# A two-layer block of linear attention and an fp8 product on one core: the last full unit's bias and final sums on DVE instead of POOL, and new orders of work at both ends

## The reference

```python
x = x + attn(layernorm(x))
x = x + ffn(layernorm(x))

def attn(h):                       # 8 heads of 16 features
    q, k, v, gate = h @ Wq.T, h @ Wk.T, h @ Wv.T, h @ Wg.T
    q, k = rope(q), rope(k)
    kv, ksum, vsum = einsum("bshd,bshe->bhde", k, v), k.sum(1), v.sum(1)
    o = (q @ kv * scale + vsum) / (q @ ksum * scale + 256)
    o = o + depthwise_conv5(v, lepe_w) + lepe_b
    return (o * gate) @ Wo.T

def ffn(h):
    xq = (h.astype(bf16).astype(f32) / s_in).astype(float8_e4m3fn)
    kq = (kernel.astype(f32) / s_k).astype(float8_e4m3fn)
    y = (xq.astype(f32) @ kq.astype(f32)) * (s_in * s_k)
    return y.astype(bf16) + bias
```

## Time and profile before

| | |
|---|---|
| median of 3 runs | 168.14 us |
| the profiled execution, its own time | 168.33 us |
| its span, first to last instruction | 166.5 us |
| PE / DVE / POOL / ACT busy | 151.4 / 149.5 / 136.1 / 125.9 us |
| granted TensorE clock, mean | 0.975 of full |

### The profile page before, as it was taken

How to read it: one execution, slowest core, us unless ns; L and a number is a source line. 1 busy time by engine, 2 the same in 40 slices (tenths; PEclk the granted TensorE clock), 3 DMA queues, 4 the chain that set the end, 5 groups by cost and what they waited for, 6 DMA issues and landing times.

```text
span 166.5 us, 3690 instructions
## 1 busy us (share of the span) xinstructions
PE 151.4 (91%) x1052; PEld 123.3 (74%) x1052; DVE 149.5 (90%) x281; ACT 125.9 (76%) x342; POOL 136.1 (82%) x164
## 2 busy tenths in 40 slices
PE   7687999999999999999999999999999999987520
PEld 2365898796877889797988888879979787865300
DVE  1269999999899999999999999999999999999563
ACT  3748857566888888989989898798687977672851
POOL 1426986866899999999989899999879989889860
PEclk9999999999999999999999999999999999999955
DMA  4955030222061915065625536263405131514223
GB/s 128 286 145 136 0 67 2 58 43 63 10 150 32 246 27 140 5 150 137 162 65 129 155 95 194 35 159 85 108 7 122 36 74 23 128 33 99 77 61 112
DMA packets 29286, 15.74 MB, mean 95 GB/s; under 512 B 9680, under 2 KB 26960, under 8 KB 29264
## 3 DMA queue, kind: packets, MB, share of 16 engines
q1 hardware_dynamic: 28688, 15.22, 36.8%
q10 hardware_dynamic: 576, 0.26, 0.6%
HBM read 5.25 MB, written 4.19 MB: 57 GB/s over the span
## 4 chain that ended last, share of the span: by engine, by line
PE 78%; DVE 5%; POOL 5%; issue 4%; SPq 3%; DMA 3%; ACT 1%; POOLq 0%; DVEq 0%; ACTq 0%
PE bank L1284 9%; PE bank L1275 8%; PE p_num L1331 8%; PE bank L1294 8%; PE bank L1320 8%; PE p_num L1339 8%; PE bank L1358 7%; PE bank L1302 7%; PE bank L1310 4%; PE bank L1348 4%; PE bank L1267 4%; DMA w_raw<-in_L_attn_Wo_dram 3%; DVE acc L982 2%; PE bank L1400 2%; POOL yc L724 1%
## 5 line engine op out<-in xcount | busy, mean ns | idle before, releaser
L982 DVE SCALAR_TENSOR_TENSOR acc<-bank,conv_w,acc 128x510 f32<-128x510 f32 (+1 forms) x48 | 34.6, 721 | 0.4 <-ACT acc L433 0.2
L394 ACT ACTIVATE h<-xs,nmr,rs 128x128 f32<-128x128 f32 x64 | 26.2, 481 | 1.2 <-POOL nmr L664 1.2
L452 ACT ACTIVATE h<-x,nmr,rs 128x128 bf16<-128x128 f32 x60 | 24.6, 483 | 2.1 <-POOL nmr L675 1.5
L708 POOL TENSOR_TENSOR k<-k_turned 128x512 f32<-128x512 f32 x16 | 20.4, 1274 | 4.2 <-DVE k_turned L967 4.2
L661 POOL TENSOR_TENSOR rs<-ve,minus_half 128x4 f32<-128x4 f32 (+1 forms) x17 | 16.6, 977 | 8.2 <-ACT ve L385 8.2
L717 POOL TENSOR_TENSOR acc<-acc,outer 128x508 f32<-128x508 f32 x16 | 20.3, 1270 | 1.1 <-DVE acc L982 1.1
L672 POOL TENSOR_TENSOR rs<-ve,minus_half 128x4 f32<-128x4 f32 (+1 forms) x17 | 16.6, 975 | 5.7 <-ACT ve L443 5.7
L701 POOL TENSOR_TENSOR qT<-q_turned,q_swapped 128x512 f32<-128x512 f32 x16 | 20.4, 1274 | 0.6 <-DMA q_swapped<-q_turned 0.6
L967 DVE TENSOR_TENSOR k_turned<-bank,turn_k 128x1024 f32<-128x1024 f32 x16 | 19.5, 1222 | 0.8 <-PE bank L1284 0.6
L955 DVE TENSOR_TENSOR q_turned<-bank,turn_q 128x1024 f32<-128x1024 f32 x16 | 19.4, 1214 | 0.0
L1320 PEld LDWEIGHTS bank<-v,k 128*128 128x128 f32 x128 | 16.5, 190 | 3.5 <-issue 3.3
(11 more groups left out here) (90 smaller groups left out, 338.1 us busy)
## 6 DMA issues: line engine op xcount, KB each, us to landing
q_swapped<-q_turned SPq DMA_DIRECT2D x32, 128.0 KB, 2.4
xs<-_attn_hidden_states_dram SPq DMA_DIRECT2D x15, 256.0 KB, 3.7
out_dram<-ob SPq DMA_DIRECT2D x15, 256.0 KB, 2.7
xs<-_attn_hidden_states_dram SPq DMA_DIRECT2D x2, 128.0 KB, 2.7
turn_q<-in_turn_q_dram SPq DMA_DIRECT2D x1, 256.0 KB, 4.0
turn_k<-in_turn_k_dram SPq DMA_DIRECT2D x1, 256.0 KB, 4.3
out_dram<-ob SPq DMA_DIRECT2D x2, 128.0 KB, 1.8
h2T<-h SPq DMA_TRANSPOSE x14, 2.5
```

Of the source, the lines that this page charges most:

```text
L394: last = nc.scalar.activation(h[:, s, t], xs[:, u % NX, t], ACT.Identity, scale=rs1[:, s, t:t + 1], bias=nmr1[:, s, t:t + 1])
L452: last = nc.scalar.activation(h2[:, s3, t], x2[:, u % 4, t], ACT.Identity, scale=rs2[:, s, t:t + 1], bias=nmr2[:, s, t:t + 1])
L708: nc.gpsimd.tensor_tensor(k[:, u % 3], k_turned[:, s, :, :, 0:D // 2], k_turned[:, s, :, :, D // 2:D], ALU.add).then_inc(k_done, 1)
L982: nc.vector.scalar_tensor_tensor(out=part, in0=p_vT[:, :, lo + off:hi + off], scalar=conv_w[:, k:k + 1], in1=part, op0=ALU.mult, op1=ALU.a ...
```

## The change

The bias sum and the final sum of unit 14 leave POOL, where they were the last two rows of its list, and stand on DVE, around `end_norm2`. They signal `late_yc_done` and `late_ob_done`, so that DVE's count and POOL's are not mixed, and `store(14)` waits for the second. The lists of calls at the start (units 0 to about 6) and at the end (units 9 to 15) are written anew on all five engines; so are the PSUM banks of a few pieces of the first and the last unit. No operation is added or dropped.

```diff
+        late_yc_done = sem("late_yc_done")
+        late_ob_done = sem("late_ob_done")
...
-                sp.wait_ge(ob_done, count(u))
+                if u == LAST - 1:
+                    sp.wait_ge(late_ob_done, 1)
+                else:
+                    sp.wait_ge(ob_done, count(u))
...
+            def add_bias(u):
+                s = u % 2
+                dve.wait_ge(yb_done, count(u))
+                dve.wait_ge(ob_done, count(u, 2))
+                nc.vector.tensor_tensor(yc[:, s], yb[:, s], fb[:].unsqueeze(1).to_broadcast([P, TPU, D]),
+                                        ALU.add).then_inc(late_yc_done, 1)
+
+            def final_sum(u):
+                dve.wait_ge(late_yc_done, 1)
+                dve.wait_ge(ob_free[u % 3], 16 * (u // 3) + 16)
+                nc.vector.tensor_tensor(ob[:, u % 3], x2[:, u % 4], yc[:, u % 2], ALU.add).then_inc(late_ob_done, 1)
...
             stats2(15, 1)
+            add_bias(14)
             end_norm2()
+            final_sum(14)
             end_quantise_if_wide(is_small)
...
             project_v(0)
             turn_weights_o((v_ready, 1), (g_ready, 1))
-            project_q(0, (hT_done, count_first(0, j=1)))
-            transpose_v(0, (hT_done, count_first(0, j=0)))
+            project_q(0)
             project_k(0, (v_done, count(0)))
+            transpose_v(0)
+            project_g(0)
             sum_v(0, (qk_ready, 1), (o_ready, 1))
-            project_g(0)
             transpose_h(1, (q_turned_done, count(0)))
-            project_k(1, (k_turned_done, count(0)))
-            key_value(0)
+            key_value(0, (hT_done, count_first(0, j=1)))
             project_q(1, (hT_done, count_first(1)))
-            project_v(1, (k_turned_done, count(1)))
+            project_v(1, (k_turned_done, count(0)))
             attend(0)
+            transpose_h(2, (q_turned_done, count(1)))
+            project_k(1, (v_done, count(1)))
```

More of the change, by code:

```diff
@@ L538, in _ @@
             norm1(5)
+            var_eps2(2)
             quantise_if_small(1, is_small)
-            var_eps2(2)
             move_hT(5)
             move_y(1)
-            for t in range(6, 9):
+            norm2(2)
+            move_v(5)
+            var_eps1(6)
+            conv_middle(5)
+            conv_outer(5)
+            quantise_if_small(2, is_small)
+            norm1(6)
+            var_eps2(3)
+            move_hT(6)
+            move_y(2)
+            for t in range(7, 12):
                 norm2(t - 4)
@@ L553, in _ @@
                 move_hT(t)
[L554 to L584, removed]
             var_eps1(12)
+            move_v(11)
             norm2(8)
-            move_v(11)
+            norm1(12)
+            conv_middle(11)
+            conv_outer(11)
@@ L737, in _ @@
             pow1(2)
+            add_q(0)
+            round_ffn_weights()
+            sum_outer(0)
+            add_k(1)
             pow1(3)
-            add_q(0)
-            add_k(1)
-            sum_outer(0)
-            round_ffn_weights()
             add_q(1)
+            sum_outer(1)
+            add_k(2)
+            pow2(0)
             pow1(4)
-            pow2(0)
-            add_k(2)
-            sum_outer(1)
             add_q(2)
             sum_outer(2)
+            add_q(3)
             add_k(3)
+            add_bias(0)
             pow2(1)
-            add_q(3)
+            final_sum(0)
             pow1(5)
-            add_bias(0)
             sum_outer(3)
             add_k(4)
-            final_sum(0)
             pow2(2)
+            add_q(4)
             add_bias(1)
-            add_q(4)
             final_sum(1)
@@ L763, in _ @@
             sum_outer(4)
-            for t in range(7, 12):
+            add_k(5)
+            pow2(3)
+            add_q(5)
+            add_bias(2)
+            final_sum(2)
+            pow1(7)
+            sum_outer(5)
+            for t in range(8, 11):
                 add_k(t - 2)
@@ L771, in _ @@
                 sum_outer(t - 2)
+            add_k(9)
+            pow2(7)
+            add_bias(6)
+            add_q(9)
+            pow1(11)
+            final_sum(6)
+            sum_outer(9)
             add_k(10)
             pow2(8)
+            pow1(12)
             add_bias(7)
-            pow1(12)
             add_q(10)
             final_sum(7)
+            add_k(11)
             pow1(13)
-            add_k(11)
+            pow1(14)
             sum_outer(10)
             pow2(9)
+            add_q(11)
+            add_k(12)
+            sum_outer(11)
             add_bias(8)
-            add_q(11)
             final_sum(8)
-            sum_outer(11)
-            add_k(12)
-            pow1(14)
             add_q(12)
+            pow1(15)
             pow2(10)
@@ L1140, in _ @@
             divide(9)
+            stats1(12)
             conv_tap(10, 2)
@@ L1477, in _ @@
             transpose_h(6, (q_turned_done, count(5)))
-            for t in range(7, 12):
+            project_g(4, (x2_done, count_last(3)))
+            key_value(5, (kvs_done, count(4)))
+            transpose_t1(4, (t2_done, count_last(3)))
+            project_v(6, (yb_done, count(2)))
+            project_q(6, (hT_done, count_first(6)))
+            transpose_v(6, (tap_done[-1], count(5)))
+            project_k(6, (v_done, count(6)))
+            project_o(4, (oT_done, count_last(4)))
+            sum_v(5, (t1_done, count_last(4)))
+            ffn(3, is_small, (k_turned_done, count(6)))
+            attend(5)
+            transpose_h(7, (q_turned_done, count(6)))
+            for t in range(8, 12):
                 project_g(t - 3, (x2_done, count_last(t - 4)))
```

346 lines of the change are left out of this document (169 added, 177 removed).

## The result

The changed kernel takes 169.36 us, the median of 4 runs (169.06 to 169.54), against 168.18 for the kernel before on the same chip: a ratio of 1.0074, interval 1.0058 to 1.009. It is slower by 1.2 us, where 2 us of gain were forecast. Its profiled execution took 169.38 us, with a span of 167.5.

The account below looks back on a forecast made before the run. PE and DVE were taken to share the bound, saturated in the middle, so only start and end could win. Gains of 1.0 + 0.95 = 1.95 us off the profiled 168.33 gave 166.4, as a median 166.2; range 164.7 to 167.6.

Parts of the forecast that it names:

- Where the time is decided: Whole kernel: the middle keeps 8.77 us per unit and gives nothing; only start and end can win.
- Term 1, the start: Start: DVE loses idle time and PE reaches transpose_t1(3) at 49.4 instead of 50.35; gain 1.0 us, bounds 0 and 1.5.
- costs nothing as long as the swap lands by 16.3: Start, SP's queue: load_x(5) may pass swap_q(0) at no cost if the swap lands by 16.3, when POOL is free.
- rounding ahead of `add_k(1)` and `pow1(3)`: Start, POOL: rival that the moved rounding delays norm1(3) and PE's transpose_h(3), losing 2.5 us: 168.7; chance 0.09.
- Between: Units 10 to 15: PE waits 0.25 and 0.35 late; DVE's last statistics end about 156.3 instead of 156.97.
- the end gains nothing: End: rival that late waits of PE or ACT give the end's gain back: 167.1; chance 0.17.
- Term 2, the hold at the end: End: POOL's unit 13 pair holds DVE once per instruction; end_norm2 ends about 160.3 instead of 161.25, gain 0.95 us.
- The rival in which DVE is not held: End: add_bias(14) gets in before POOL's pair and keeps its place; term 2 is 2.4, time 164.7; chance 0.12.
- Whichever goes first: End, DVE: one instruction waits behind each POOL instruction in any order, so end_norm2 ends at about 160.3.

Follow-up runs that it names:

- mended_start: Kernel before with the new start, DVE's load of the flag ahead of invert(2), load_x(5) behind swap_q(0); old end, sums on POOL: 167.34 us.
- both_first: Changed kernel with DVE's load of the flag ahead of invert(2) and load_x(5) behind swap_q(0): 168.21 us.
- swap_first: Changed kernel with only load_x(5) put back behind swap_q(0) in SP's list: 168.64 us.
- load_first: Changed kernel with only DVE's load of the flag put ahead of invert(2): 168.35 us.
- q8_early: both_first with quantise(8) and quantise(9) ahead of the convolutions of units 11 and 12 in ACT's list: 168.18 us.
- h_first: both_first with end_norm2 ahead of add_bias(14) in DVE's list: 167.71 us, ratio 0.9975.
- pair13_waits: both_first with POOL's add_bias(13) and final_sum(13) waiting until DVE's end_norm2 has ended: 168.61 us.
- new_start: Kernel before with the new lists of all engines up to the steady middle, old end with sums on POOL: 168.26 us, ratio 1.0008.

## Why the prediction was wrong, point by point

In sum: against the forecast 166.2 the kernel is 3.2 us late. The two waits of the start are 1.15 of this, and the start's order itself is 0.14 short. The end is 1.8: it cost 0.87 us (from `mended_start`, 167.34, to `both_first`, 168.21), where a gain of 0.95 was forecast.

- **Where the time is decided** was right: the period stayed, the ends decided, and what a start gains is carried through (`mended_start` keeps 0.86 to the end).
- **Term 1, the start, -1.0**, was right for the order itself (-0.86, with `transpose_t1(3)` at 49.47) and wrong as a whole, since two steps were costed at nothing. The first is the sentence that `load_x(5)` ahead of `swap_q(0)` "costs nothing as long as the swap lands by 16.3". Its condition was named and never checked. Behind a 256 KB load the swap landed 4.3 us after its issue, at 16.9, and POOL was free for `add_q(0)` at 15.7, not at 16.3. `swap_first` takes it away: 0.7.
- The second is the flag's load on DVE. The prediction has no step for it: the walk took "the durations of the rows", and the load has no row. It cost 0.78 at the row, and up to 1.0 in the time (`load_first`, where the swap came earlier as well). A bound from the trace was there: `turn_k` of 1.22 us in front of it hid all of it.
- The **rounding ahead of `add_k(1)` and `pow1(3)`**, the slower rival, did not come: `norm1(3)` ended at 27.63, 0.3 later than walked, and that is inside the wait for the swap. The side of the result was given 0.09 for another mechanism than the one that came.
- **Between** is the step of the end that failed. Late waits of PE were walked as 0.25 and 0.35, and DVE was to end the last statistics 0.65 earlier than with the old order. With the same start it ends them 0.67 later (156.66 against 155.99): 1.3 of the 1.8 us. DVE waits 1.97 us for PE there, where its waits in `mended_start` are 1.39 in all. As a step of its own the new order of units 9 to 15 costs 0.73. Waits for PE are the mechanism of the rival "the end gains nothing", but it went beyond that rival's price: the end does not give its gain back, it loses. That rival's other half, `quantise` on ACT, was tried for units 8 and 9 in `q8_early` and gave nothing back.
- **Term 2, the hold at the end,** was right in its mechanism: POOL's pair holds DVE once behind each of its two instructions. It was also in the sum, so it explains little of the miss: from the end of the last statistics to that of `end_norm2` the forecast has 4.0 us (156.3 to 160.3), the changed kernel 4.45. What the prediction missed is that the change itself put the pair of unit 13 there. That place costs 1.30. The sums' own move is worth 1.16 to 1.28 where POOL is quiet, and 0.25 at most where it is not. The old end order with the sums moved, which the prediction never priced, is the better kernel. The rival in which DVE is not held did not come either.
- "**Whichever goes first**" was wrong by up to half a microsecond, and that is most of the other 0.45 of the end. In `h_first` it takes 4.12 us from the last statistics (156.51) to the end of `end_norm2` (160.63), and the kernel is 0.5 faster. Two instructions are held in either order, but with `add_bias(14)` first the second instruction of `end_norm2` stands third and runs after the hold, and the chain waits for it.

What stays open is which calls of units 9 to 15, or which of the new banks, make the 0.73. Two candidates were tried, and neither alone gives it back; perhaps more than one wait has to go at once, since a removed wait came back each time elsewhere. This was not tried.

## What to carry to other kernels

Price a new order against the old order with the wanted edit alone: here the edit gained 1.2 us, and the new order of the end around it lost 2.0. In a walk over lists, count what has no busy row as well (a register load, a DMA's place in its queue), and look for the long instruction that hides it now. Where two engines hold each other, move the other engine's work out of the stretch before moving work into it.

## What the runs showed that was not expected

- A register load on DVE: some 0.8 us of standing still when only a 0.35 us instruction lies before it (37.92 to 38.70), nothing to be seen behind one of 1.22 us (`load_first`).
- The hold goes both ways. In `pair13_waits` POOL's bias sum started at 159.37 beside DVE's `final_sum(14)`, which had begun at 159.21, and took 1.53 us instead of 1.15. The Trainium skill, SBUF — State Buffer, "SBUF: two separate sides", calls the port pair that DVE and POOL share an exclusive lock: of a POOL instruction and a DVE instruction in a 2-port mode or with two SBUF inputs, whichever starts first keeps it for the whole instruction. The traces agree: DVE's 0.42 became 1.38 beside a POOL instruction of 1.15 that had started 0.05 earlier.
- A transfer of 128 KB of a swap takes 2.4 us from issue to landing in the median of before (2.2 to 4.0). That of unit 0, directly behind a 256 KB load, took 4.3 us in the changed kernel and in `new_start`, but at most 3.5 in `load_first` with the same order.
- Two waits of 1.0 and 0.7 us, taken away together, gave 1.15, not 1.7. That the profile of `load_first` has less of the other wait as well may be why; it was not shown.
